# A ViT tower on one core: the second turning of x and a weighing moved on TensorE, the last rows' scores moved on VectorE

## Chip, cores and metric

The kernel runs on one core of one Trainium2 chip. The metric is the time on the device in microseconds, the median of some runs. Times below are microseconds unless ns is written. PE is TensorE (PEld its weight loads), DVE is VectorE, ACT is ScalarE, POOL is GpSimd, SP is the sync engine, which issues most DMAs.

## What is computed

One layer of a vision tower on 32 images of 128 tokens and one class token, 1024 features, in float32:

```
h  = S4D kernels from x, log_dt, A, B               (32, 128, 1024)     "mix"
h  = concat([cls_tok, h], axis=1)                   (32, 129, 1024)
xn = layernorm(h);  q, k, v = xn@Wq.T, xn@Wk.T, xn@Wv.T      32 heads, 8 for k and v, of 32
q, k = rope(q), rope(k);  p = softmax(causal(q k^T / sqrt(32)));  h = h + (p v) @ Wo.T
xn = layernorm(h);  h = h + quant8_per_token(xn) @ quant8_per_channel(w).T + b
```

## The kernel before

Three stages follow each other: the mix (0 to about 165 us), attention (to about 1025 us) and the FFN (to the end). Each engine has its own queue, written out by hand, and the queues meet in semaphores. The order of the work is the order of the code in each engine's `body(t)`.

**Attention** handles one tile (one image, 128 tokens) per `body(t)`; each body has 8 steps `s`. Several tiles are in work at once: in the body of t, the rows of n = t+1 are normalised and turned, q, k and v of t are projected, the scores and the softmax of b = t-1 are made, and its weighing with v belongs to c = t-2 (softmax lags by steps: `group_at(t, s, lag)` gives the group of four heads that is due). The bodies of tiles 4 to 29 run in a hardware loop, the first and last are written out.

- Projection (line 1098): 72 matmuls of 128x128x512 a tile, nine in each step: four at its head (`ahead = 4`), five at its end. float32 is split in two parts (`xT_hi`, `xT_lo`; `w_hi`, `w_lo`) and three products are made.
- `turn_x(n, r)` (line 1130): four transposes of `xn` into one PSUM bank, rounds r = 0 and 1. ACT's `split_x` (1229) casts the bank to `xT_hi`, then DVE's `split_x` (1349) makes `xT_lo` from the bank and `xT_hi` and increments `x_lo`. `x_bank` names the bank: Y_BANK (ps 5) for both rounds, except in the first tiles. `x_steps` gives the steps, 6 and 7.
- `scores` (1141) at steps 1 and 5, each 32 matmuls into four banks. They need q, which is turned (1122) through Y_BANK and copied by ACT (`store_q`, 1215) at steps 0 and 3, and k (1109, 1209).
- On DVE `mask` (1392), `row_maximum` (1401), `inverse` (1408), `part_turned` (1385, the 32x32 transposing of p); on ACT `exponentials` (1223); on POOL `normalise_p` (979). SP writes p in parts to DRAM (`part_p`, 876) and reads it back whole (`whole_p`, 886). `part_turned` of group g waits for the parts of group g-2.
- `weigh(c, half)` (1153) multiplies p with v into C_BANK (ps 4) at steps 3 and 7. ACT's `context` (1248) copies the bank to `ctxo`, SP stores it (844), and POOL's `save_ctx` (984) keeps its last column. At step 7 of POOL, `save_ctx` stands ahead of the normalising of the next step.

In step 7, TensorE issued four projections, `turn_x(n, 1)`, `weigh(c, 1)` and five projections.

**FFN** runs one tile per body too: `project` (1747, 48 matmuls with Wo) of tile t, then `dense_layer` (1839, 16 matmuls) of tile c = t-1 on the int8 values. On DVE a tile's residual and statistics (1884, 1886) come once its projection ends, then `quantise` (1912 to 1925); SP turns the rows with a DMA (1628) before the dense layer. For the first three tiles the projection is made ahead, in the attention stage's last bodies. In between, the last token of all 32 images (it has a 129th key) is handled apart: `end_scores` (1961 to 1969), `end_weights`, `end_context` on DVE.

## Time and profile before

| | |
|---|---|
| runs | 1484.79, 1489.23, 1493.75 us; median 1489.23 |
| profiled execution | 1493.45 us, span of the core 1491.6 us |
| PE busy | 1428.2 us (96%) |
| DVE busy | 1160.9 us (78%) |
| POOL busy | 921.2 us (62%) |
| ACT busy | 734.1 us (49%) |
| DMA | 255.60 MB, mean 171 GB/s |

The profile is of one execution. A chain of work that ended last is followed back from the last instruction; 79% of it lies on PE. Matmuls are pipelined: one starts while the last still runs, so the distance of starts counts, not the duration. A releaser of a wait is inferred from semaphores; "issue" means that none was found.

### The profile page before, as it was taken

To read this page: it belongs to the slowest core of one execution; us is meant where nothing else is said; L and a number is where in the kernel's file an instruction comes from. 1 tells how busy PE (TensorE), PEld (TensorE's weight loads), DVE (VectorE), ACT (ScalarE), POOL (GpSimd) and SP (SyncE) were. 2 spreads that over 40 slices of the span, in tenths; PEclk is the share of its full clock that TensorE was granted. 3 is DMA by queue.
4 is the path that set the end of the run, shared out by engine and by line. 5 is a ranking of instruction groups with operands and counts; after the bars stand their busy time and mean duration, and the time that the engine had idled before them with its cause. 6 is when DMAs were issued, how large, how long until landed. Compare 5 with 4: busy or idle time off the path is not lost.

```text
span 1491.6 us, 34063 instructions
## 1 busy us (share of the span) xinstructions
PE 1428.2 (96%) x10442; PEld 1109.5 (74%) x10442; DVE 1160.9 (78%) x2285; ACT 734.1 (49%) x2673; POOL 921.2 (62%) x958
## 2 busy tenths in 40 slices
PE   5999888999999999999999999889999999999997
PEld 3999866777777777777777777676677777777774
DVE  7888678789999999999999998787765655656555
ACT  6897566576767676676767676562000000000000
POOL 5796156576767767676767767445555556455552
PEclk8999999999999999999999999999999999999998
DMA  9356666677767777777767776867434344343442
GB/s 236 102 142 152 191 142 164 181 191 204 202 200 205 201 210 194 209 194 203 200 196 206 198 206 189 259 207 200 149 113 148 116 130 134 112 145 116 133 113 60
DMA packets 264458, 255.60 MB, mean 171 GB/s; under 512 B 73329, under 2 KB 201586, under 8 KB 264402
## 3 DMA queue, kind: packets, MB, share of 16 engines
q1 hardware_dynamic: 257586, 233.87, 56.4%
q10 hardware_dynamic: 6816, 21.04, 4.7%
q8 instruction: 29, 0.48, 0.1%
q14 instruction: 27, 0.22, 0.1%
HBM read 138.26 MB, written 106.57 MB: 164 GB/s over the span
## 4 chain that ended last, share of the span: by engine, by line
PE 79%; DVE 7%; POOL 6%; DMA 3%; issue 2%; SPq 2%; ACT 1%; ACTq 0%; DVEq 0%; POOLq 0%
PE att_ps L1098 33%; PE ffn_o L1747 22%; PE ffn_y L1839 7%; PE att_ps L1141 4%; PE att_ps L1153 4%; POOL yb L358 3%; PE att_ps L1130 2%; PE att_ps L1122 2%; POOL yb L364 2%; PE mix_ps L447 1%; DMA p_blocks<-pB 1%; SPq L876 1%; PE att_ps L1109 1%; DMA xqT<-xq 1%; DVE m L641 1%
## 5 line engine op out<-in xcount | busy, mean ns | idle before, releaser
L1223 ACT ACTIVATE pr<-sm,ml 128x128 f32<-128x128 f32 x1024 | 399.1, 393 | 164.6 <-DVE ml L1401 163.3
L979 POOL TENSOR_TENSOR pr<-pr,ri 128x512 f32<-128x512 f32 x256 | 266.9, 1043 | 206.9 <-DVE ri L1408 199.8
L1098 PE MATMUL att_ps<-w_lo,xT_hi 128*128 128x512 f32 x776 | 319.9, 412 | 0.0
L1098 PE MATMUL att_ps<-w_hi,xT_hi 128*128 128x512 f32 x776 | 312.5, 403 | 3.9 <-DVE xT_lo L1349 3.1
L1098 PE MATMUL att_ps<-w_hi,xT_lo 128*128 128x512 f32 x776 | 307.6, 396 | 0.0
L1801 ACT CAST cT_hi<-ctx_in 128x512 fp32r<-128x512 f32 x64 | 36.4, 616 | 363.1 <-PE ffn_o L1747 350.8
L1747 PE MATMUL ffn_o<-wo_hi,cT_hi 128*128 128x512 f32 x528 | 211.8, 401 | 2.3 <-DVE wo_lo L1790 1.7
L1392 DVE TENSOR_TENSOR sm<-att_ps,cst 128x512 f32<-128x512 f32 x256 | 170.0, 664 | 51.9 <-PE att_ps L1141 51.9
L1747 PE MATMUL ffn_o<-wo_hi,cT_lo 128*128 128x512 f32 x528 | 205.7, 390 | 0.0
L1747 PE MATMUL ffn_o<-wo_lo,cT_hi 128*128 128x512 f32 x528 | 205.4, 389 | 0.0
L1223 ACT ACTIVATION_READ_ACCUMULATOR pr<-sm,ml 128x1 f32 x1024 | 193.4, 189 | 0.0
L1385 DVE STREAM_TRANSPOSE pB<-pr 128x512 f32<-128x512 f32 x256 | 176.3, 689 | 21.8 <-DMA p_blocks<-pB 19.6
L1401 DVE TENSOR_REDUCE ml<-sm 128x4 f32<-128x512 f32 x256 | 176.1, 688 | 9.1
L1098 PEld LDWEIGHTS att_ps<-w_hi,xT_hi 128*128 128x128 f32 x776 | 146.1, 188 | 41.2 <-issue 2.9
L1098 PEld LDWEIGHTS att_ps<-w_lo,xT_hi 128*128 128x128 f32 x776 | 146.6, 189 | 39.1 <-issue 12.5
L1098 PEld LDWEIGHTS att_ps<-w_hi,xT_lo 128*128 128x128 f32 x776 | 146.7, 189 | 28.6
L1884 DVE TENSOR_TENSOR h<-ffn_o,h_in 128x512 f32<-128x512 f32 x66 | 45.5, 690 | 148.1 <-PE ffn_o L1747 148.1
L1720 POOL TENSOR_TENSOR hb<-h,bias_sb 128x512 f32<-128x512 f32 x66 | 85.5, 1295 | 95.1 <-DVE xq L1925 60.6
L1839 PE MATMUL ffn_y<-wq,xqT 128*128 128x512 bf16 x528 | 124.9, 392 | 10.1 <-DMA xqT<-xq 10.1
L965 POOL TENSOR_SCALAR xn<-hbuf,mv,rstd 128x512 f32<-128x512 f32 x64 | 133.3, 2083 | 0.2
L1747 PEld LDWEIGHTS ffn_o<-wo_hi,cT_hi 128*128 128x128 f32 x528 | 99.2, 188 | 26.3 <-issue 3.6
L447 PE MATMUL mix_ps<-eb,m 128*128 128x128 f32 x1024 | 116.1, 275 | 1.0 <-DVE m L632 0.6
(212 smaller groups left out, 2340.7 us busy)
## 6 DMA issues: line engine op xcount, KB each, us to landing
pT<-p_blocks SPq DMA_DIRECT2D x256, 256.0 KB, 2.9
p_blocks<-pB SPq DMA_DIRECT2D x512, 64.0 KB, 2.0
h_rows<-ho SPq DMA_DIRECT2D x64, 256.0 KB, 3.8
ctx_turned<-ctxo SPq DMA_DIRECT2D x64, 256.0 KB, 3.6
h_in<-h_rows SPq DMA_DIRECT2D x32, 512.0 KB, 3.7
out_dram<-yo SPq DMA_DIRECT2D x32, 512.0 KB, 2.7
ctx_in<-ctx_turned SPq DMA_DIRECT2D x30, 512.0 KB, 3.3
hbuf<-h_rows ACTq DMA_DIRECT2D x29, 512.0 KB, 4.7
```

Source lines behind the costliest of these rows:

```text
L447: mm = nc.tensor.matmul(bank[:, cols], term[:, half, h, slots].rearrange("p j c -> p (j c)"), eb[:, k % 3, half * CH + h, :], start=term i ...
L965: G.tensor_scalar(xn[:, cols], hbuf[:, n[1], cols], mv[:, 0:1], rstd[:], ALU.subtract, ALU.mult).then_inc(xn_ready, 1)
L979: G.tensor_tensor(pr[:, g % 4], pr[:, g % 4], ri[:, g % 2, :].unsqueeze(2).to_broadcast([P, GQ, P]), ALU.mult).then_inc(p_ready, 1)
L1098: mm = nc.tensor.matmul(bank[:], x_part[:, t[1], e, tok:tok + P], w_part[blk][:, e, :], start=(r == 0), stop=(r == EC * 3 - 1))
L1141: mm = nc.tensor.matmul(S_BANK[j][:, q * P:(q + 1) * P], qT[rows, half, q, :], kT[rows, b[1], half, :], start=True, stop=True)
L1223: a = nc.scalar.activation(pr[:, g % 4, q, :], sm[:, g % 2, q, :], ACT.Exp, bias=ml[:, b[1], 0, h:h + 1], accum_out=ml[:, b[1], 1, h:h + 1])
L1385: V.transpose(pB[:, g % 2].rearrange("p k h f -> p h k f"), pr[:, g % 4].rearrange("p h (k f) -> p h k f", k=4)).then_inc(p_turned, 1)
L1392: V.tensor_tensor(sm[:, g % 2], S_BANK[g % 4][:].rearrange("p (q k) -> p q k", q=GQ), cst[:, C_MASK:C_MASK + P].unsqueeze(1).to_broadcast( ...
L1401: V.tensor_reduce(ml[:, b[1], 0, heads_of(g)], sm[:, g % 2], AX.X, ALU.max, negate=True).then_inc(negmax_ready, 1)
L1720: done = nc.gpsimd.tensor_tensor(hb[:, t[1], cols], h1[:, t[1], cols], bias_sb[:, cols], ALU.add)
L1747: mm = nc.tensor.matmul(O_BANK[half][:], c_part[:, t[1], e, :], w_part[:, e, half * BK:(half + 1) * BK], start=(r == 0), stop=(r == PER_HA ...
L1839: mm = nc.tensor.matmul(Y_BANK[half][:], xqT[:, c[1], e, :], wq8[:, e, half * BK:(half + 1) * BK], start=(e == 0), stop=(e == EC - 1))
```

## The change

Five things change in attention. (1) Round 1 of every tile's x goes to C_BANK. (2) From tile 1 on, `turn_x(n, 1)` comes at the end of step 6 instead of the middle of step 7; it now waits for the first context of tile n-3 to be out of the bank. (3) `weigh(c, 1)` goes to the end of step 7, behind its five projections, and waits for both splits of tile n. (4) DVE makes both splits of x at one place, before the mask of step 7; ACT copies the context of half 1 behind the exponentials of step 7. (5) SP stores that half at step 0 of the next body, behind `part_p` and `whole_p`. In the FFN, (6) DVE makes `end_scores` in the body of tile 2, behind `quantise`, instead of at the end of the body of tile 1.

```diff
     def x_bank(n, r):
 
-        return C_BANK if r == 1 and fixed(n) and nth(n) <= 2 else Y_BANK
+        return C_BANK if r == 1 else Y_BANK
...
     def x_steps(n):
 
-        return (3, 4) if at(n, 0) else (6, 7)
+        return (3, 4) if at(n, 0) else (6, 7) if last_rows(n) else (6, None)
...
                 if s == 1 and exists(c, NB):
                     store_ml(c)
-                if s == 7 and exists(c, NB):
+                if s == 0 and exists(shifted(t, -3), NB):
+                    store(shifted(t, -3), 1)
+                if s == 7 and at(t, NB + 1):
                     store(c, 1)
...
         def turn_x(n, r):
             pe.wait_ge(xn_ready, XROUNDS * nth(n) + r + 1)
-            at_least(pe, x_lo, 2 * nth(n) + (r if x_bank(n, r) is Y_BANK else 0))
+            at_least(pe, x_lo, 2 * nth(n))
             at_least(pe, k_stored, number(n))
+            if r == 1 and exists(shifted(n, -3), NB):
+                pe.wait_ge(ctx_ready, 2 * number(shifted(n, -3)) + 1)
...
             at_least(pe, ctx_ready, 2 * u + half)
+            if half == 1 and exists(shifted(b, 3), NB):
+                pe.wait_ge(x_lo, 2 * nth(shifted(b, 3)) + 2)
...
-                if s == 7 and exists(c, NB):
-                    weigh(c, 1)
                 for r in rounds_at(t, s):
                     pe_round(pe, r)
                 if has_rows(t):
                     project(t, min(s * per_step + ahead, count), min((s + 1) * per_step, count))
+                if s == 6 and has_rows(n) and x_steps(n)[1] is None:
+                    turn_x(n, 1)
+                if s == 7 and exists(c, NB):
+                    weigh(c, 1)
...
                 for r in range(XROUNDS):
-                    if s == x_steps(n)[r] and has_rows(n):
+                    if s == (x_steps(n)[r] or 7) and has_rows(n):
                         split_x(n, r)
-                if s == 7 and exists(c, NB):
-                    context(c, 1)
...
                 if exists(d, NB):
                     exponentials(d, g)
+                if s == 7 and exists(c, NB):
+                    context(c, 1)
...
-                if s == x_steps(n)[1] and has_rows(n):
+                if s == (x_steps(n)[1] or 7) and has_rows(n):
                     split_x(n, 0)
+                    if x_steps(n)[1] is None:
+                        split_x(n, 1)
...
             if exists(t, NT):
                 quantise(t)
+            if at(t, 2):
+                end_scores()
             for half in range(2):
                 if exists(c, NT):
                     scale_out(c, half)
                 if last_rows(c):
                     add_last(c, half)
-            if at(t, 1):
-                end_scores()
```

TensorE's queue in the loop, steps 6 and 7 of a body, before (ps 4 is the contexts' bank, ps 5 the other; in brackets the semaphores waited for):

```order
L1098 MATMUL att_ps7<-w_hi2,xT_lo 128x512
L1098 MATMUL att_ps7<-w_hi2,xT_hi 128x512
L1130 MATMUL att_ps5<-cst,xn 128x128 [waits att_k_stored,att_x_lo,att_xn_ready]
L1130 MATMUL att_ps5<-cst,xn 128x128 x3
L1153 MATMUL att_ps4<-pT,v_sb 32x128 [waits ctx_ready,att_v_moved,att_p_whole1]
L1153 MATMUL att_ps4<-pT,v_sb 32x128 x15
L1098 MATMUL att_ps7<-w_lo2,xT_hi 128x512
```

And now (lines are the changed kernel's; seven of the nine projections between are left out):

```order
L1100 MATMUL att_ps7<-w_lo2,xT_hi 128x512
L1100 MATMUL att_ps7<-w_hi2,xT_lo 128x512
L1134 MATMUL att_ps4<-cst,xn 128x128 [waits att_k_stored,ctx_ready,att_x_lo,att_xn_ready]
L1134 MATMUL att_ps4<-cst,xn 128x128 x3
...
L1100 MATMUL att_ps7<-w_lo2,xT_hi 128x512
L1100 MATMUL att_ps7<-w_hi2,xT_lo 128x512
L1159 MATMUL att_ps4<-pT,v_sb 32x128 [waits ctx_ready,att_x_lo,att_v_moved,att_p_whole1]
```

The second turning stands four projections earlier, without need of the first round's split, and the weighing nine projections behind it, with `x_lo` as a new wait.

ScalarE's queue at the same place, before and now (the register rows belong to waits and the loop):

```order
L1223 ACTIVATE pr,ml<-sm,ml 128x128 x4
L1228 REGISTER_ALU
L1229 CAST xT_hi<-att_ps5 128x4x128
L1248 COPY ctxo<-att_ps4 128x512
L1219 REGISTER_ALU
L1223 ACTIVATE pr,ml<-sm,ml 128x128 x4
L816 REGISTER_ALU
L816 COMPARE_AND_BRANCH
L1215 COPY qT<-att_ps5 128x512
L1223 ACTIVATE pr,ml<-sm,ml 128x128 x12
```

```order
L1231 ACTIVATE pr,ml<-sm,ml 128x128 x4
L1236 REGISTER_ALU
L1237 CAST xT_hi<-att_ps4 128x4x128
L1227 REGISTER_ALU
L1231 ACTIVATE pr,ml<-sm,ml 128x128 x4
L1256 COPY ctxo<-att_ps4 128x512
L816 REGISTER_ALU
L816 COMPARE_AND_BRANCH
L1223 COPY qT<-att_ps5 128x512
L1231 ACTIVATE pr,ml<-sm,ml 128x128 x12
```

The copy of the context, which stood ahead of step 7's four exponentials, stands behind them, right before the copy of q (`qT`).

VectorE's queue in the FFN, bodies of tiles 1 and 2, before and now:

```order
L1925 TENSOR_SCALAR xq<-xr 128x1024
L1935 SCALAR_TENSOR_TENSOR ya<-ffn_y,xs,w_scale 128x512 x2
L1961 TENSOR_TENSOR prod<-ffn_c,k_end 32x512 x2
L1965 TENSOR_REDUCE s_end<-prod 32x32
L1967 SCALAR_TENSOR_TENSOR nm_end<-s_end,ml_end 32x32
L1968 TENSOR_TENSOR w_end<-nm_end,ml_end 32x32
L1969 TENSOR_TENSOR w_end<-nm_end,s_end 32x32
L1884 TENSOR_TENSOR h<-ffn_o,h_in 128x512
L1886 BN_STATS ffn_st<-h 128x6
```

```order
L1945 SCALAR_TENSOR_TENSOR ya<-ffn_y,xs,w_scale 128x512 x2
L1894 TENSOR_TENSOR h<-ffn_o,h_in 128x512
...
L1935 TENSOR_SCALAR xq<-xr 128x1024
L1971 TENSOR_TENSOR prod<-ffn_c,k_end 32x512 x2
L1975 TENSOR_REDUCE s_end<-prod 32x32
L1977 SCALAR_TENSOR_TENSOR nm_end<-s_end,ml_end 32x32
L1978 TENSOR_TENSOR w_end<-nm_end,ml_end 32x32
L1979 TENSOR_TENSOR w_end<-nm_end,s_end 32x32
L1945 SCALAR_TENSOR_TENSOR ya<-ffn_y,xs,w_scale 128x512 x2
L1983 TENSOR_TENSOR e_end<-e_end,ml_end 32x32
```

The five instructions of the last rows' scores (`prod` to `w_end`) stood between the scaling of tile 0 and the residual of tile 2; now they stand behind tile 2's quantising (`xq`).

## Rows read from the trace of the kernel before

**Rows 1.** The page, busy time of the matmuls over the whole span
```profile
PE 1428.2 (96%) x10442; PEld 1109.5 (74%) x10442; DVE 1160.9 (78%) x2285; ACT 734.1 (49%) x2673; POOL 921.2 (62%) x958
```

**Rows 2.** Waits of 320 to 900 us: total, times, longest
```profile
DVE sm L1392 <- PE att_ps L1141: 38.6, 48, 0.9
...
PEld att_ps L1130 <- issue: 13.8, 24, 1.2
```

**Rows 3.** Timeline of PE, one tile: start, duration (us), instruction
```profile
581.93 1.17 PE L1141 MATMUL att_ps<-kT,qT 32*128 32x128 f32 x32
...
597.67 0.60 PE L1130 MATMUL att_ps<-cst,xn 128*128 128x128 f32 x4
...
598.34 0.39 PE L1098 MATMUL att_ps<-w_hi,xT_lo 128*128 128x512 f32 x1
...
599.96 0.40 PE L1098 MATMUL att_ps<-w_hi,xT_hi 128*128 128x512 f32 x1
600.52 0.63 PE L1130 MATMUL att_ps<-cst,xn 128*128 128x128 f32 x4 [0.16 <-issue]
...
606.00 1.17 PE L1141 MATMUL att_ps<-kT,qT 32*128 32x128 f32 x32
```

**Rows 4.** Timeline of DVE, the same tile
```profile
599.76 0.65 DVE L1349 TENSOR_TENSOR xT_lo<-att_ps,xT_hi 128x512 fp32r<-128x512 f32 x1
...
601.80 0.69 DVE L1349 TENSOR_TENSOR xT_lo<-att_ps,xT_hi 128x512 fp32r<-128x512 f32 x1
...
607.34 0.69 DVE L1392 TENSOR_TENSOR sm<-att_ps,cst 128x512 f32<-128x512 f32 x1 [0.92 <-PE att_ps L1141]
```

**Rows 5.** Timeline of ACT, the same tile
```profile
598.79 0.40 ACT L1223 ACTIVATE pr<-sm,ml 128x128 f32<-128x128 f32 x1
...
600.25 0.19 ACT L1223 ACTIVATION_READ_ACCUMULATOR pr<-sm,ml 128x1 f32 x1
...
602.22 0.59 ACT L1248 COPY ctxo<-att_ps 128x512 f32<-128x512 f32 x1 [0.46 <-PE att_ps L1153]
...
605.03 0.59 ACT L1215 COPY qT<-att_ps 128x512 f32<-128x512 f32 x1 [0.67 <-PE att_ps L1122]
```

**Rows 6.** Timeline of POOL, the same tile
```profile
602.98 0.19 POOL L984 COPY c_end<-ctxo 128x4 f32 x1 [1.38 <-ACT ctxo L1248]
603.13 1.04 POOL L979 TENSOR_TENSOR pr<-pr,ri 128x512 f32<-128x512 f32 x1
```

**Rows 7.** Chain that ended last, first tiles: start, us, what
```profile
282.35 2.27 issue
...
309.88 1.19 issue
```

**Rows 8.** Busy time by stretches: length, PE, PEld, DVE, ACT, POOL, granted clock, DMA
```profile
283.00:290.00 7.00, 5.38 (x48) 4.17 (x49) 6.30 (x13) 3.41 (x14) 3.51 (x4) 0.76 0.51 135
...
1049.00:1057.00 8.00, 7.28 (x25) 3.23 (x26) 7.02 (x13) 0.00 (x0) 2.33 (x3) 0.58 0.36 135
```

**Rows 9.** Timeline of PE, dense layers of FFN tiles 2 and 3
```profile
1049.72 6.56 PE L1839 MATMUL ffn_y<-wq,xqT 128*128 128x512 bf16 x16 [2.83 <-DMA xqT<-xq]
...
1067.93 3.63 PE L1839 MATMUL ffn_y<-wq,xqT 128*128 128x512 bf16 x16
```

**Rows 10.** Timeline of DVE, start and end of the last rows' scores
```profile
1031.97 1.27 DVE L1961 TENSOR_TENSOR prod<-ffn_c,k_end 32x512 f32<-32x512 f32 x2
...
1034.94 0.67 DVE L1884 TENSOR_TENSOR h<-ffn_o,h_in 128x512 f32<-128x512 f32 x1
```

**Rows 11.** Timeline of SP, turned rows of FFN tiles 2 and 3 issued
```profile
1043.14 1.67 SPq L1628 DMA_TRANSPOSE xqT<-xq  x1
...
1058.66 1.24 SPq L1628 DMA_TRANSPOSE xqT<-xq  x1
```

**Rows 12.** Landing of the turned rows (line 1628), 1010 to 1120 us
```profile
DMA to landing us min/median/max: 4.1/5.0/6.7
```

**Rows 13.** Landing of the parts of p (line 876), 320 to 900 us
```profile
DMA to landing us min/median/max: 1.7/2.1/2.9
```

## The prediction

> **What bounds the kernel now.** I read the page first: the matmuls are busy 96% of the span [rows 1], so the time is the length of TensorE's own queue plus the holes in it. Then the waits of 320 to 900 us, the regular part of the attention stage (24 tiles): there TensorE has one hole of size per tile, before a turning of x (line 1130), 13.8 us in 24 times as its weight loads show it, and VectorE waits twice per tile for the scores, 0.8 us a time [rows 2]. So TensorE leads, and VectorE follows with little slack.
>
> The timeline of one tile shows the hole. The reader is to see where the even step breaks: seven projection matmuls lie between 598.34 and 599.96, so one takes 0.231 us. The next instruction should begin at 600.19, and the second turning begins at 600.52 [rows 3]. It writes the bank that VectorE reads in its first split of x, from 599.76 to 600.41 [rows 4], and starts 0.11 us behind it. The hole is 0.33 us, and "issue" in the brackets hides that it is a semaphore of VectorE. From scores to scores, 581.93 to 606.00, a tile takes 24.07 us [rows 3].
>
> The first tiles are worse: the same place costs 2.27 us and two tiles later 1.19 us in the chain [rows 7] (the tile before the former lost 2.03 alike, the one behind the latter 0.81). After the long one the granted clock of the next 7 us averages 0.76, that is a time at 1.2 instead of 2.4 GHz [rows 8]; after the one of 1.19 the turning ran at its full speed.
>
> **The change in a steady tile, step by step.** (1) The second turning goes to the contexts' bank, so it no longer waits for the first split. The 0.33 us are gone on TensorE. It also moves four matmuls ahead, to 600.19 - 4 x 0.231 = 599.27. Its other waits are met: the bank's earlier content is copied out and xn normalised microseconds before.
>
> (2) The weighing now comes nine matmuls later. A turning between two projections costs 598.34 - 597.67 - 0.231 = 0.44 us [rows 3], so it wants to start at 599.27 + 0.44 + 9 x 0.231 + 0.08 = 601.87. It waits for VectorE's second split. ScalarE casts that half behind its exponentials, 0.09 us after 600.25, for 0.59 us [rows 5], so until 600.93; the split then ends at 600.95 + 0.69 = 601.64 (0.69 from [rows 4]). That is 0.2 us early, so I cost it at nothing; it is the thinnest cover here.
>
> (3) VectorE does both splits in a row and idles for the cast from 600.41 to 600.95. From the first split's start to the second's there were 2.04 us in the trace [rows 4]: the split (0.6), a mask and a row maximum (1.4). Both now come behind the second split, whose successor starts 0.6 us after it, at 601.56: the row maximum ends at 602.96, where VectorE was free again at 601.80 + 0.61 = 602.41 with the split done. So the rest of its queue shifts by some 0.45 us on its own account: it had finished a transposing of p (0.68 us) at 607.34 - 0.92 = 606.42 [rows 4] and now would at 606.87.
>
> (4) ScalarE's four exponentials of step 7 start at 603.0. A group takes 600.25 + 0.09 - 598.79 = 1.55 us [rows 5]; then the context is copied (one copy follows another after 0.48 us), and the copy of q starts at 605.03. Today it starts at 605.03 too, waiting for TensorE [rows 5]. So q is stored at 605.6, and the scores can start at 605.66, where TensorE's own path alone gives 606.00 - 0.33 = 605.67 or a little less. Two chains end together; the gain is 0.34 us at most, if nothing adds.
>
> (5) POOL still saves a column of the context in step 7, and behind it in its queue stands the normalising of p. Today the column is saved at 602.98, 0.17 us behind the copy's end, and p normalised from 603.13, for 1.04 us [rows 5, 6]; now the copy ends at 605.12, the column follows at 605.29, and p is normalised from 605.44 to 606.48. VectorE's transposing of that p starts at 606.52 instead of 606.19, and its mask comes 0.63 us later, at 607.15, where the earlier scores would allow 607.34 - 0.34 = 607.00 [rows 4]. That 0.15 us is taken from the 0.8 us of slack that VectorE has before the next scores [rows 2], and costs nothing.
>
> (6) On SP the store of the context's second half goes behind the parts and the whole of the next step of p. Part 5 of p is issued about 0.9 us later relative to the scores; parts land in 2.1 us, 2.9 at most [rows 13], and VectorE needs it 3 us after its issue has ended. Nothing.
>
> The new waits on registers (ctx_ready at the turning, x_lo at the weighing) have no row; the nearest is the weights' idle time of a turning without a hole, under 0.1 us. Between 0 and 0.2 us per tile, I take 0.04. So **0.30 us a tile**, 25 tiles: 7.5 us. Bounds: 0.41 us (TensorE alone, if q comes earlier) and 0.10.
>
> (7) The first four tiles that the new bank reaches. In the second, the old turning stood from 282.35 to 284.62. The weighing would stand 0.44 + 5 x 0.231 = 1.6 us behind the old place, at 283.95, and its split ends 0.6 us behind the old release, at 285.2. So 1.2 us of waiting remain of 2.27, and the clock should stay up, as it did after 1.19 us. The low clock cost 7 x (1 - 0.76) = 1.7 us [rows 8], so 2.8 us come back, less what step (4) takes: 2.5 here, and 2.5 in the tile before. In the next two the weighing finds its split done and the stalls of 1.19 and 0.81 go: 1.9 us. Together **6.9 us** (bounds 4 and 7.5; the lower one if the clock still falls).
>
> (8) The last attention tile runs into a stretch where VectorE is bound by the landing of p's parts; there part 5 is late by what steps (3) and (5) add. **Minus 0.4 us.**
>
> **The scores of the last rows.** Their five instructions hold VectorE from 1031.97 to 1034.94 [rows 10], ahead of the residual, statistics and quantising of the third tile, and its dense layer waits for exactly that: TensorE idles 2.83 us until 1049.72 [rows 9]. Moved behind, they take 2.97 us off this way. SP issued the turned rows at 1043.14 [rows 11]; its queue has a few small loads first, so 1040.6. The dense layer starts at 1047.1, 2.6 us earlier. Its 16 matmuls took 6.56 us at a mean clock of 0.58 where the next tile's took 3.63 [rows 8, 9]; with an idle time under 1 us they should run at full speed: 2.9 us more, 5.5 in all. But it isn't all kept. VectorE's sum of work up to the fourth tile's quantising is unchanged, so its turned rows still leave at 1058.66 [rows 11] and land 4.1 to 6.7 us later, 5.0 in the middle [rows 12]: at 1063.7. TensorE now arrives at 1067.93 - 5.5 = 1062.4. It waits 1.3 us; **4.3 us** stay. Bounds: 5.5 (landing in 4.1), and nothing, if they land in 6.7 at 1065.4 and the dense layer falls to the low clock again (2.5 less 2.9).
>
> Here a rule speaks against the change. The trace shows that the clock fell after idle times of 2.27 and 2.83 us and not after 1.19 [rows 7 to 9], and my sum keeps it up in both places. The Trainium skill, page "TensorE: Matmul & The Clock Gate", Part 1, has the gate follow how busy the array has recently been, not one idle time; by that, several short holes in a row could bring it down as one long one does.
>
> **The sum.** 7.5 + 6.9 - 0.4 + 4.3 = 18.3 us. The profiled execution took 1493.45 us, so 1475.1 for its like; the median of the runs is 1489.23, so **1471 us**.
>
> **Rivals.** (A) ScalarE's chain sets the tile. If steps (3) and (4) take 0.3 us more than counted (a wait's latency on each of four hand-overs), the scores start where they do today and the steady gain is nil; the copy of q was waiting for TensorE until now, which speaks against it, the exact tie for it. 4.0 + 3.0 = 7 us: 1482. 15%.
> (B) The clock rule above: the holes of 1.2 and 1.3 us still bring it down. 4.0 of 6.9 and 1.4 of 4.3 stay: 7.5 + 4.0 - 0.4 + 1.4 = 12.5 us: 1477. 10%.
> (C) Slower: part 5 of p. In the regular stretch parts land in 2.1 us, but in the first tiles VectorE did wait for them. If the later issue makes it wait, each tile loses what exceeds 0.9 + 0.8 us of slack; at a landing of 4.8 us that is 1.0 us a tile, 25 us, against 18 gained: 1496. It decides from a landing of about 4 us; the longest in 24 tiles was 2.9. 4%.
> (D) The hole is not the split but the sequencer working through waits ("issue"). Then the change gives only the scores' 4.3 us and adds two waits at 0.1 us to 30 tiles: 1488. Against it: the first turning has the same three waits and no hole. 3%.
>
> **Chances.** Forecast 68%, A 15, B 10, C 4, D 3. A measurement of this kernel tells 0.5%, 7.4 us, from no change (the limit is 1481.8). Faster: forecast, B and half of A, 0.86. Same: the other half of A and D, 0.10. Slower: C, 0.04. The range runs from all upper bounds, 0.41 x 25 + 7.5 + 5.5 = 23 us and some spread of the runs, 1463, to A's far end, 1484.
>
> **What would show it.** No idle time before the second turning; the weighing 0 to 0.2 us behind its place; the copy of q at the same distance from its scores as TensorE's arrival; a tile of 23.77 us instead of 24.07; 0.3 us waits of VectorE for POOL's p; the clock at 1.00 in the second tile and in the dense layer of the third; the dense layer near 1047 minus what the attention stage saved. A tile of 24.0 or more, with TensorE waiting for the copy of q, would make A right; a wait of VectorE for parts of p in most tiles, C.

## The result, and the profile after

| | before | changed |
|---|---|---|
| median of 8 runs each | 1489.22 us | 1477.13 us |
| lowest and highest | 1484.79, 1493.75 | 1475.51, 1481.45 |
| profiled execution (span) | 1493.45 (1491.6) | 1476.76 (1475.0) |
| PE busy | 1428.2 us | 1418.8 us |

The ratio is 0.9921, 95% interval 0.9905 to 0.9938: the change saves 12 us, 9 to 14 by the interval. The same kernel on another chip, beside the last two experiments, gave 0.9917 (0.9894 to 0.9940). The forecast was 1471 us with a range of 1463 to 1484: faster was right, the range holds it, and the gain is a third smaller than the forecast's 18.3.

TensorE's matmuls cover 96% of the span as before [rows 1]:

```profile
PE 1418.8 (96%) x10442; PEld 1109.0 (75%) x10442; DVE 1162.4 (79%) x2285; ACT 725.4 (49%) x2673; POOL 920.2 (62%) x958
```

**The steady tiles.** The waits of 320 to 900 us, by engine and line: us in total, times, the longest. They answer to [rows 2].

```profile
POOL c_end L986 <- ACT ctxo L1256: 83.1, 24, 3.7
...
DVE sm L1400 <- PE att_ps L1145: 11.5, 25, 0.7
...
PEld att_ps L1145 <- ACT qT L1223: 8.9, 24, 0.5
DVE pB L1393 <- POOL pr L981: 7.8, 24, 0.4
DVE xT_lo L1357 <- ACT xT_hi L1237: 7.3, 17, 0.5
DVE pB L1393 <- DMA p_blocks<-pB: 3.9, 14, 0.4
```

The wait of the turning's weights ("issue", 13.8 us in 24 times) is gone, and VectorE waits for the scores 11.5 us instead of 38.6: it has lost two thirds of its slack. In its place stand two small waits that the forecast had named: VectorE's for POOL's p (7.8 us in 24 times, 0.33 a time) and its wait for the cast of x's second half (7.3 us in 17 times).

One tile of TensorE, as in [rows 3]; a line is a group's start, its duration and the instruction:

```profile
583.98 1.17 PE L1145 MATMUL att_ps<-kT,qT 32*128 32x128 f32 x32
...
590.03 0.60 PE L1134 MATMUL att_ps<-cst,xn 128*128 128x128 f32 x4
...
592.65 1.08 PE L1159 MATMUL att_ps<-pT,v_sb 128*32 128x128 f32 x32
...
594.69 0.60 PE L1124 MATMUL att_ps<-cst,rsq 128*128 128x128 f32 x4
...
596.38 1.17 PE L1145 MATMUL att_ps<-kT,qT 32*128 32x128 f32 x32
```

No idle time stands behind any of them: TensorE's queue of the tile has no hole left. The second turning at 590.03 used to wait for a split; the weighing at 592.65 finds its split done, though only just (the splits, two of them, end at 590.87 + 1.48 = 592.35 in the row below). ScalarE, POOL and VectorE beside it, each with its own idle time in brackets [rows 4 to 6]:

```profile
593.71 0.40 ACT L1231 ACTIVATE pr<-sm,ml 128x128 f32<-128x128 f32 x1 [2.08 <-DVE ml L1409]
...
595.26 0.56 ACT L1256 COPY ctxo<-att_ps 128x512 f32<-128x512 f32 x1
595.73 0.58 ACT L1223 COPY qT<-att_ps 128x512 f32<-128x512 f32 x1
```

```profile
595.99 0.19 POOL L986 COPY c_end<-ctxo 128x4 f32 x1 [3.28 <-ACT ctxo L1256]
596.14 2.04 POOL L981 TENSOR_TENSOR pr<-pr,ri 128x512 f32<-128x512 f32 x2
```

```profile
590.87 1.48 DVE L1357 TENSOR_TENSOR xT_lo<-att_ps,xT_hi 128x512 fp32r<-128x512 f32 x2
...
597.22 0.71 DVE L1393 STREAM_TRANSPOSE pB<-pr 128x512 f32<-128x512 f32 x1 [0.22 <-POOL pr L981]
```

The copy of q starts at 595.73, ends at 596.31, and its scores start at 596.38, the tie of step (4). Before, ScalarE stood idle ahead of that copy and waited for TensorE (0.67 us in [rows 5]); that wait is gone from the list. The matmuls don't wait there. Their weight loads wait for ScalarE, 8.9 us in 24 times in the waits above, but in the kernel before it was 8.7 in 24 times, so that wait says nothing of the tie; the experiment context_first below does. POOL sits idle for 3.28 us until the context is copied, and VectorE's transposing waits 0.22 us for the p behind it, as step (5) has it.

A tile's length is best taken over many. The group of 32 scores is issued 64 times; from the 13th to the 59th lie 23 tiles:

| | 13th scores | 59th scores | us a tile |
|---|---|---|---|
| before | 365.33 | 918.81 | 24.06 |
| changed | 359.38 | 904.53 | 23.70 |

The gain is 0.36 us a tile, 8.3 us over these 23. Of it 0.33 us is the hole. Another 0.03 is the second turning itself: its four transposes take 0.60 us now (590.03 above) and took 0.63 behind the hole [rows 3]. In the two further traces with the old attention it came back as 24.05, in the five further ones with the changed attention as 23.70 each time.

**The first tiles.** TensorE's largest hole there is now this, and the clock behind it is the second row (columns as in [rows 8]):

```profile
282.51 1.08 PE L1159 MATMUL att_ps<-pT,v_sb 128*32 128x128 f32 x32 [2.14 <-DVE xT_lo L1357]
```

```profile
282.00:290.00 8.00, 7.49 (x82) 5.93 (x83) 6.45 (x14) 4.25 (x18) 4.56 (x6) 0.79 0.76 223
```

It is the hole that the forecast wanted to shrink to 1.2 us, and the clock fell as in the kernel before. VectorE is late for it by waits of its own, in the 10 us ahead:

```profile
273.39 0.71 DVE L1393 STREAM_TRANSPOSE pB<-pr 128x512 f32<-128x512 f32 x1 [1.85 <-POOL pr L981]
...
277.24 0.71 DVE L1393 STREAM_TRANSPOSE pB<-pr 128x512 f32<-128x512 f32 x1 [1.75 <-DMA p_blocks<-pB]
...
281.12 1.25 DVE L1357 TENSOR_TENSOR xT_lo<-att_ps,xT_hi 128x512 fp32r<-128x512 f32 x2
```

**The last rows' scores.** TensorE's dense layers of FFN tiles 2 and 3, then VectorE's quantising and scores, then SP's queue and the landing of the turned rows of tile 2. They answer to [rows 9 to 12].

```profile
1035.38 5.02 PE L1849 MATMUL ffn_y<-wq,xqT 128*128 128x512 bf16 x16 [4.91 <-DMA xqT<-xq]
...
1052.05 3.63 PE L1849 MATMUL ffn_y<-wq,xqT 128*128 128x512 bf16 x16
```

```profile
1023.58 0.69 DVE L1935 TENSOR_SCALAR xq<-xr 128x1024 bf16<-128x1024 f32 x1
1024.18 1.27 DVE L1971 TENSOR_TENSOR prod<-ffn_c,k_end 32x512 f32<-32x512 f32 x2
...
1034.58 0.69 DVE L1894 TENSOR_TENSOR h<-ffn_o,h_in 128x512 f32<-128x512 f32 x1
```

```profile
1019.47 3.34 SPq L1673 DMA_DIRECT2D ctx_last_rows<-cls_value  x4
1022.91 1.48 SPq L1599 DMA_DIRECT2D ctx_in<-ctx_turned  x1
1024.50 0.87 SPq L1604 DMA_DIRECT2D h_in<-h_rows  x1
1025.43 3.72 SPq L1638 DMA_TRANSPOSE xqT<-xq  x1
```

```profile
DMA to landing us min/median/max: 9.9/9.9/9.9
```

The scores (1024.18) did leave the way of the quantising (1023.58). But the turned rows, which landed 6.5 us after their issue in the kernel before, now need 9.9, and TensorE idles 4.91 us instead of 2.83. The dense layer took 5.02 us instead of 6.56. Set against the last weighing, at 1024.85 before and 1010.25 now, tile 2's dense layer starts after 24.87 us before and 25.13 now, so no sooner, and tile 3's after 43.08 and 41.80. The stretch is 1.3 us shorter, and what made it so is that tile 2's matmuls ran 1.5 us faster, not that they began earlier.

### The profile page after: what moved, and what is told of

Its sections match the earlier page's. It is cut to its first block, busy times and chain, and to the rows that moved or that the text cites. A ratio compares the mean times of both kernels' runs of the same rounds, so it can differ in the third digit from the quotient of the medians.

```text
span 1475.0 us, 34108 instructions
## 1 busy us (share of the span) xinstructions
PE 1418.8 (96%) x10442; PEld 1109.0 (75%) x10442; DVE 1162.4 (79%) x2285; ACT 725.4 (49%) x2673; POOL 920.2 (62%) x958
## 4 chain that ended last, share of the span: by engine, by line
PE 72%; DVE 8%; POOL 6%; DMA 4%; SPq 4%; issue 3%; ACT 2%; ACTq 0%; DVEq 0%; POOLq 0%
PE att_ps L1100 30%; PE ffn_o L1757 21%; PE ffn_y L1849 7%; PE att_ps L1145 4%; PE att_ps L1159 3%; POOL yb L358 3%; SPq L876 3%; DMA p_blocks<-pB 2%; PE att_ps L1124 2%; POOL yb L364 2%; PE att_ps L1134 2%; PE mix_ps L447 1%; DMA xqT<-xq 1%; DVE sm L1400 1%; DVE pB L1393 1%
## 5 line engine op out<-in xcount | busy, mean ns | idle before, releaser
L1100 PE MATMUL att_ps<-w_hi,xT_hi 128*128 128x512 f32 x776 | 318.9, 411 | 2.6 <-DVE xT_lo L1357 2.0
L1100 PE MATMUL att_ps<-w_lo,xT_hi 128*128 128x512 f32 x776 | 316.5, 408 | 0.0
L1894 DVE TENSOR_TENSOR h<-ffn_o,h_in 128x512 f32<-128x512 f32 x66 | 45.5, 690 | 147.8 <-PE ffn_o L1757 147.7
L1757 PEld LDWEIGHTS ffn_o<-wo_hi,cT_hi 128*128 128x128 f32 x528 | 99.2, 188 | 25.3 <-ACT wo_hi L1795 1.8
```

Of the source, the lines that this page charges most:

```text
L1100: mm = nc.tensor.matmul(bank[:], x_part[:, t[1], e, tok:tok + P], w_part[blk][:, e, :], start=(r == 0), stop=(r == EC * 3 - 1))
L1757: mm = nc.tensor.matmul(O_BANK[half][:], c_part[:, t[1], e, :], w_part[:, e, half * BK:(half + 1) * BK], start=(r == 0), stop=(r == PER_HA ...
```

## The experiments

Eleven kernels ran in three groups, each group beside runs of the kernel before on its chip (their medians: 1491.1, 1491.4 and 1490.4 us). Besides the ratio I read two lengths from each trace, which scatter less than the time: the steady tile, and the way from the start of the last weighing to tile 3's dense layer, called the FFN way below.

| kernel | median, us | ratio (95%) | steady tile | FFN way |
|---|---|---|---|---|
| before, profiled with the result | 1489.22 | 1 | 24.06 | 43.08 |
| changed, profiled with the result | 1477.13 | 0.9921 (0.9905 to 0.9938) | 23.70 | 41.80 |
| changed_again | 1478.05 | 0.9917 (0.9894 to 0.9940) | 23.70 | 42.67 |
| scores_back | 1479.21 | 0.9928 (0.9908 to 0.9948) | 23.70 | 43.65 |
| scores_only | 1492.64 | 1.0004 (0.9986 to 1.0021) | 24.05 | 40.97 |
| copies_later | 1475.57 | 0.9901 (0.9880 to 0.9923) | 23.70 | 37.41 |
| copies_later_again | 1474.97 | 0.9901 (0.9879 to 0.9923) | 23.70 | 37.68 |
| before_copies_later | 1486.78 | 0.9976 (0.9962 to 0.9989) | 24.05 | 37.42 |
| copies_scores_back | 1476.15 | 0.9897 (0.9872 to 0.9921) | 23.70 | 38.36 |
| turning_later | 1493.18 | 1.0011 (0.9996 to 1.0025) | 24.24 | 42.14 |
| context_first | 1480.90 | 0.9919 (0.9897 to 0.9941) | 23.77 | 43.80 |
| save_later | 1479.45 | 0.9924 (0.9899 to 0.9948) | 23.70 | 42.32 |
| two_products_out | 1469.58 | 0.9844 (0.9820 to 0.9868) | 23.32 | 42.04 |

In the traces of the last four kernels of the table the record of a dense layer's first matmul is missing, so that their FFN way is read one matmul, 0.23 us, too long.

My theory after the result: the attention part of the change works by taking every hole out of TensorE's queue; the scores' move works too, but its gain is lost to the landing of the turned rows, which is set by four copies of small pieces queued ahead of them on SP (line 1673). The rivals are the forecast's own figure (4.3 us for the scores) and, for the attention, that VectorE or ScalarE sets the tile.

### The two parts, each by itself

scores_back takes one part out of the changed kernel, scores_only puts it alone into the kernel before:

```
-            if at(t, 2):
-                end_scores()
             for half in range(2):
...
+            if at(t, 1):
+                end_scores()
```

> The changed kernel with the last rows' scores back behind the second tile's scaled product; the change to the attention stays. The forecast's theory (the scores' move is worth 4.3 us, since xqT of tile 2 lands as much earlier as it is issued earlier) gives 1477.1 + 4.3 = 1481.4 us. My theory now: the landing is bound by what is queued ahead of it, the four copies of cls_value into ctx_last_rows and then ctx_in and h_in (xqT landed 9.9 us after its issue in the changed kernel, 6.5 us before), so that an issue 2 to 3 us later lands at the same moment, the dense layer of tile 2 still starts about 1035.4 us and the time is 1477 to 1479 us. In the trace: landing of that xqT near 7 us instead of 9.9.

> The kernel before with the scores' move alone. The forecast's theory: 1489.2 - 4.3 = 1484.9 us. My theory now (landing bound by the small copies ahead of it): 1487.5 to 1489.2 us, and xqT of tile 2, issued about 1040.5 us instead of 1043.1, lands about 9 us later, at the moment at which it landed before.

The part back, the ratio is 0.9928 against 0.9921; alone, it is 1.0004. By both, the scores are worth nothing that the times can tell, and 4.3 us of 1489 is a ratio of 0.9971, outside scores_only's interval. The turned rows of tile 2 landed 8.2 us after their issue in scores_back, 8.7 in scores_only. I had expected 7 and 9: the issue that comes later does land faster, but not by as much. The FFN ways say the same: 43.65 to 41.80 and 42.67 in the changed kernel (1.4 us), 43.08 to 40.97 in the kernel before (2.1 us), where 4.3 was forecast. These sizes are rough. Three kernels below have the FFN of the changed kernel too, context_first, save_later and two_products_out, and their ways are 43.6, 42.1 and 41.8 (less the 0.23 us named under the table), so that one trace scatters by as much as what is to be measured. Tile 2's dense layer starts 25.60 us after the last weighing in scores_back and 25.0 to 26.0 in the five traces with the attention changed and the scores moved: the move doesn't bring it forward. All this also shows that nearly the whole measured gain is the attention's.

### The copies ahead of the turned rows

```
-            if at(t, 2):
+            if at(t, 3):
                 sp.wait_ge(v0_out, 16)
                 for q in range(GQ):
                     sp.dma_start(tail_dram[NB:P].rearrange("t (g q d) -> t g q d", g=HKV, q=GQ)[:, :, q, :],
```

> The changed kernel with the four copies of cls_value into ctx_last_rows issued one tile later, behind the turning of tile 2's xq. My theory: ctx_in, h_in and xqT are no longer queued behind them, xqT of tile 2 is issued about 1 us earlier (1024.4) and lands in 4 to 5 us as the others do, before tile 2's projection ends (1030.5), so the dense layer starts with no hole (4.9 us in the changed kernel), at full clock (3.6 us instead of 5.0). That is up to 4.9 + 1.4 = 6.3 us; some of it can be lost to the wait of the tile after: 1471 to 1474 us. Rival: the landing is long because of ctx_in and h_in themselves (1 MB ahead of it) and the copies cost nothing: 1477 us, landing still 8 us or more.

> The kernel before with only the four copies of cls_value issued one tile later. My theory: xqT of tile 2, issued at 1043.1 us as before, lands after 4.4 us instead of 6.5, the hole ahead of the dense layer shrinks from 2.8 to 0.7 us and its clock stays full (3.6 us instead of 6.6): 2.1 + 2.9 = 5 us, 1484 to 1486 us. Rival (the copies cost nothing): 1489 us.

The four copies are of 96 KB each, in pieces of 32 floats (128 bytes). The same stretch of SP and TensorE with them behind:

```profile
1020.29 0.37 SPq L1599 DMA_DIRECT2D ctx_in<-ctx_turned  x1
1025.06 0.33 SPq L1604 DMA_DIRECT2D h_in<-h_rows  x1
1025.43 1.25 SPq L1638 DMA_TRANSPOSE xqT<-xq  x1
...
1032.28 3.43 SPq L1673 DMA_DIRECT2D ctx_last_rows<-cls_value  x4
```

```profile
DMA to landing us min/median/max: 4.4/4.4/4.4
```

```profile
1031.05 3.63 PE L1849 MATMUL ffn_y<-wq,xqT 128*128 128x512 bf16 x16
...
1048.42 3.62 PE L1849 MATMUL ffn_y<-wq,xqT 128*128 128x512 bf16 x16 [1.15 <-DMA xqT<-xq]
```

The turned rows leave at the same moment, 1025.43, and land after 4.4 us instead of 9.9; tile 2's dense layer starts with no hole and takes 3.63 us. Why, the bandwidth shows. Here are 40 slices of 1022 to 1031 us, busy tenths of the 16 engines and GB/s, first of the changed kernel, then of copies_later:

```profile
DMA  3033323332333233223220110211222268989899
GB/s 51 13 58 50 50 48 58 61 51 48 59 61 51 48 59 60 49 48 52 43 31 15 32 25 15 36 18 23 45 45 42 39 142 261 370 327 464 346 473 401
```

```profile
DMA  7998897110000000015689896889899200200000
GB/s 200 273 382 328 328 473 310 55 55 18 0 0 0 0 0 0 0 55 127 182 309 492 273 382 218 270 231 214 162 272 298 47 0 0 73 0 0 0 0 0
```

With the copies in the queue it moves about 50 GB/s for 4.5 us, then less until 1029; the 512 KB each of ctx_in and h_in, and the turned rows behind them, wait until it is nearly over (the last copy lands at 1030.6) and then go at 260 to 470. The Trainium skill, page "DMA: Bandwidth & Descriptors", section "Queues, rings and completion order", says that each DMA engine takes the descriptors of one ring in their order; the trace agrees, since three transfers issued from 1022.9 to 1025.4 hardly move before the copies are through.

In the changed kernel this is worth 4.4 to 5.3 us of the FFN way (41.80 and 42.67 to 37.41), in the kernel before 5.7 us. In time it is 3 us: 1478.05 and 1474.97 on one chip, and 0.9901 twice against 0.9921 and 0.9917. The intervals of these overlap; that of before_copies_later against its kernel does not reach 1. The rival was that the 1 MB of loads ahead makes the landing long. The loads are still issued ahead of the turned rows, and the 512 KB of h_in only 0.37 us ahead, without harm; the 512 KB of ctx_in have landed by then, since SP gets to them sooner without the copies. So the copies are the cause, directly and by holding the loads back. How the 5 us divide between the two isn't shown.

I had expected 1471 to 1474 us for copies_later, and 1475.57 came. The next hole takes a part back, as said there: 1.15 us before tile 3's dense layer. For before_copies_later I had expected 1484 to 1486 us against 1489. 1486.78 came, against 1491.1 on that chip: 4.3 us less by the medians and 3.6 by the ratio, where 5 was expected. Its turned rows landed after 4.2 us instead of 6.5, and the dense layer took 3.63, as expected.

### Both together: what the scores' move is worth without the copies

The edits of scores_back and of copies_later in one kernel, beside the changed kernel and copies_later once more.

> The changed kernel with the four copies of cls_value one tile later and the last rows' scores back where they were. My theory: with the copies out of the way the place of the scores is worth nothing or up to 1 us, since then VectorE's and the tensor engine's own work sets the tile: tile 3's dense layer starts 37.4 to 38.4 us after the last weighing (37.4 with the copies moved alone, with either place of the scores), 1473 to 1477 us. Rival (the forecast's): the scores ahead of tile 2's quantising cost 2.6 us wherever the copies are: 40 us after the last weighing, 4.3 us more than with the copies moved alone.

> The changed kernel once more, beside the two that follow, so that they are compared on one chip. 1477 to 1480 us (0.990 to 0.994 of before); steady tile 23.70 us; xqT of tile 2 lands 9 to 10 us after its issue, and tile 3's dense layer starts 41.5 to 42.5 us after the last weighing.

> The changed kernel with the four copies one tile later, once more, beside the changed kernel: 3 to 4.5 us under it (41.8 - 37.4 = 4.4 us between the last weighing and tile 3's dense layer), 1473 to 1476 us.

The FFN way is 38.36 us, against 37.41 and 37.68: 0.7 to 1.0 us for the place of the scores, and the ratios (0.9897, 0.9901) are the same. Tile 2's dense layer has a hole of 1.95 us ahead of it, tile 3's then none. So the forecast's 4.3 us fail here too: VectorE had room for most of the 3 us of scores. The times of the other two are those expected, 3.1 us apart. The FFN way of the changed kernel again, 42.67, lies 0.2 above the stretch I had given. The turned rows landed after 10.0 us there, as in the first trace.

### The bank without the earlier place

turning_later keeps the new bank, the split of both halves in one go and the weighing at the end of step 7, but puts the turning itself back:

```
                 for r in range(XROUNDS):
-                    if s == x_steps(n)[r] and has_rows(n):
+                    if s == (x_steps(n)[r] or 7) and has_rows(n):
                         turn_x(n, r)
...
-                if s == 6 and has_rows(n) and x_steps(n)[1] is None:
-                    turn_x(n, 1)
```

> The changed kernel with x's second turning back in step 7, behind four products of the projection as in the kernel before; the bank stays the contexts', the split stays one group of two, and the weighing stays at the end of step 7. It tells the bank from the place. The turning comes four products later (some 0.95 us), about 591.0 instead of 590.0 in the tile read; ScalarE's cast then ends about 592.3 instead of 591.6, VectorE's second split about 593.0 instead of 592.3, and the weighing, which the tensor engine reaches at 592.65, waits 0.3 to 0.8 us for it; the mask behind the split is as late. My theory: the tile takes 24.0 to 24.4 us instead of 23.70 (the kernel before: 24.06), in all 8 to 17 us over the changed kernel: 1485 to 1494 us. Rival: the bank alone brings the gain, the place is indifferent: 1477 us.

```profile
DVE xT_lo L1355 <- ACT xT_hi L1235: 20.5, 24, 1.1
...
PE att_ps L1159 <- DVE xT_lo L1355: 7.9, 24, 0.3
```

24.24 us a tile, more than the kernel before (24.06). The new wait of the weighing for the second split stands in it 24 times with 0.33 us, just where the old hole of 0.33 was, and VectorE waits 20.5 us for the cast instead of 7.3. So the attention change without the earlier place is a loss of 0.18 us a tile against the kernel before; what pays is that the turning comes four products earlier, into a bank that lets it. (The kernel before with the new bank and nothing else did not run, nor did the weighing's place or the order of the splits by itself.) The 0.54 us over the changed kernel stand in two places, read from the starts of the matmuls in 23 tiles. From the last product to the weighing it is 0.72 us instead of 0.33. From the last product to the scores behind q's copy it is 0.45 instead of 0.33. The time, 1493.18 us, lies in the expected 1485 to 1494.

### Relief off TensorE, and less work on it

context_first puts ScalarE's copy of the context ahead of step 7's exponentials; save_later puts POOL's column of it behind the next normalising of p:

```
+                if s == 7 and exists(c, NB):
+                    context(c, 1)
                 for r in rounds_at(t, s):
...
                     exponentials(d, g)
-                if s == 7 and exists(c, NB):
-                    context(c, 1)
```

```
                     normalise_p(d, g)
+                if s == 0 and exists(shifted(t, -3), NB):
+                    save_ctx(shifted(t, -3), 1)
...
-                if s == 7 and exists(c, NB) and not at(c, NB - 1):
-                    save_ctx(c, 1)
```

> The changed kernel with ScalarE's context copy of the second half back ahead of step 7's exponentials. The weighing ends (593.73) just when those exponentials can start (593.71), so the copy pushes them 0.5 us back and comes 1.5 us earlier itself; the copy of q after both starts where it did. My theory: nothing changes in the steady tile (23.70 us, 0 to 0.1 more) and the time stays at 1477 to 1479 us; the order on ScalarE was indifferent, though GpSimd gets the context 1.5 us earlier and VectorE's wait of 0.22 us for pr goes. Rival: exponentials later by 0.5 us make the chain to the next scores later by as much: 24.2 us a tile, 1489 us.

> The changed kernel with GpSimd's save of the second half's last context column behind the first normalising of the next tile, so that pr no longer waits behind ctxo (3.28 us idle on GpSimd, 0.22 us on VectorE in each tile). My theory: the tensor engine has no hole left in the steady tile, so relief of VectorE and GpSimd is worth nothing there: 23.70 us a tile, 1476 to 1478 us. Rival: VectorE still sets the tile (its wait of 0.22 us is on the path): 23.48 us a tile, 24 x 0.22 = 5 us less, 1472 us.

The waits of save_later, where POOL no longer stands behind the context:

```profile
POOL c_end L986 <- ACT ctxo L1256: 26.8, 24, 1.1
DVE sm L1400 <- PE att_ps L1145: 17.6, 24, 0.8
...
DVE pB L1393 <- DMA p_blocks<-pB: 2.4, 3, 1.0
```

POOL's idle time for the context falls from 83.1 to 26.8 us, VectorE's for p (7.8 us) is gone, its wait for the scores grows from 11.5 to 17.6, and the tile stays at 23.70. The 0.22 us were slack turned into slack. (The median, 1479.45, lies above the expected 1476 to 1478; the ratio, 0.9924, is the changed kernel's.) context_first has 23.77: 0.07 more, within what I had written, so the order on ScalarE that the change brings is all but indifferent. The 0.07 stand in one place, the scores behind q's copy, which start 0.39 us after the last product instead of 0.33. There ScalarE has no slack left: the tie of step (4) is real. (Its median, 1480.9, lies above the 1479 I had given; its first scores came at 215.32 us, the latest but one of all the traces of this study, and its ratio is the changed kernel's.)

two_products_out removes work from TensorE alone, two products of the projection in each tile:

```
+                if not last_rows(t) and blk == 2 and r in (5, 8):
+                    continue
                 x_part, w_part = PARTS[part]
```

> The changed kernel with two of the 72 products of each tile's projection left out (in the third block: one of w_lo with xT_hi and one of w_hi with xT_lo are missing from q's second half), to see whether the tensor engine's queue sets the steady tile now. Each product takes 0.23 us in the queue. My theory: it does, so the tile takes 23.70 - 0.46 = 23.24 us, and over 32 tiles the time falls by 13 to 15 us, to 1462 to 1464 us; a part of it can be lost to the next engine, since VectorE's chain is only some 0.1 to 0.4 us behind. Rival: another engine (VectorE, or ScalarE's copy of q in front of the scores) sets it: 23.6 to 23.7 us a tile, 1475 to 1477 us.

```profile
L1147 PE MATMUL att_ps<-kT,qT 32*128 32x128 f32 x1600 | 58.7, 283 | 1.0
L1161 PE MATMUL att_ps<-pT,v_sb 128*32 128x128 f32 x1568 | 53.0, 275 | 1.3 <-DVE xT_lo L1359 0.9
```

23.32 us a tile: 0.38 of the 0.46 us come through, and the rest is idle time in the last column, 1.0 us before the scores and 1.3 before the weighing (0.7 of the latter in one of the first tiles). By the starts, the scores behind q's copy come 0.41 us after the last product instead of 0.33, and the weighing 0.37 instead of 0.33. So TensorE sets the tile, the rival is out, and the reserve behind it is thin: ScalarE's copy of q and VectorE's split show as soon as 0.4 us is taken. In time it is 8 us (of the medians) to 11 us (of the ratios) under the changed kernel, less than the 13 to 15 I had given, which took all 32 tiles at 0.46; 0.38 for the 24 steady ones alone gives 9.

## Why the forecast was right, and where not

**Steady tile, steps (1) to (6): right, by its own mechanism.** 0.36 us instead of 0.30, inside the bounds of 0.10 and 0.41. The hole is gone, the weighing finds its split done, ScalarE's copy of q and TensorE arrive together, and VectorE waits for POOL's p at no cost, as save_later shows. The 0.04 us I had set aside for the new waits weren't needed, and 0.03 came from the turning itself, which I had not counted. 23 tiles give 8.3 us.

**First four tiles, step (7), 6.9 us: mis-sized, about 3.9.** Here are the six tiles from the first scores to the 13th, each from scores to scores, in three traces with the old attention (before, scores_only, before_copies_later) and in six with the changed one (changed, changed_again, scores_back and the three with the copies later or both). The forecast's four tiles are numbers 2 to 5.

| tile | 1 | 2 | 3 | 4 | 5 | 6 | sum |
|---|---|---|---|---|---|---|---|
| old | 22.6, 24.1, 25.5 | 28.3, 25.0, 24.1 | 27.6, 27.9, 28.3 | 25.1, 25.0, 26.1 | 24.8, 24.2, 24.1 | 24.0, 24.1, 24.1 | 152.3, 150.2, 152.1 |
| changed | 22.3 to 23.9 | 23.8 to 24.3 | 25.3 to 27.5 | 23.9 to 25.3 | 23.7 to 25.6 | 23.7 | 144.5 to 147.7 |
| gain of the means | 1.1 | 1.8 | 1.7 | 0.4 | 0.0 | 0.4 | 5.4 |
| forecast | 0.3 | 2.5 | 2.5 | 1.9 for both | | 0.3 | 7.5 |

Two sentences failed. The larger miss is "In the next two the weighing finds its split done and the stalls of 1.19 and 0.81 go: 1.9 us." In five of the six changed traces the weighing of tile 4 waits 1.0 to 1.4 us for its split; the trace of the result, where it doesn't, is the exception. In those five VectorE had stood 1.8 to 2.1 us for the landing of p's parts some 5 us earlier, as here in copies_later:

```profile
303.70 0.71 DVE L1393 STREAM_TRANSPOSE pB<-pr 128x512 f32<-128x512 f32 x1 [2.10 <-DMA p_blocks<-pB]
```

```profile
308.97 1.08 PE L1159 MATMUL att_ps<-pT,v_sb 128*32 128x128 f32 x32 [1.38 <-DVE xT_lo L1357]
```

That the wait for the parts causes the hole is read from the order of the rows; no run took it away. The other sentence is "So 1.2 us of waiting remain of 2.27, and the clock should stay up", with 2.5 us for each of two tiles. In tile 3 the hole is 1.35 to 2.14 us, and the clock stayed at 1.00 in four of the six traces but fell in two, the trace of the result among them. And tile 2's 2.5 us were read off one execution: it took 28.3 us there, but 25.0 and 24.1 in the other two traces of the old attention. (A reading to be corrected too: the hole of 1.19 us is one tile behind that of 2.27, not two.)

**Last attention tile, step (8), minus 0.4 us: open.** From the 59th scores to the last weighing the three old traces take 106.0, 109.7 and 106.0 us, the six changed ones 104.1 to 107.6. The scatter hides it.

**The last rows' scores, 4.3 us: the step that failed.** The sentence is "its queue has a few small loads first, so 1040.6. The dense layer starts at 1047.1": it carried the landing of 6.5 us over to an earlier issue. The 6.5 was already at the far end of 4.1, 5.0 and 6.7 [rows 12], and the reason, four copies issued from 1034.97 to 1038.40 ahead of it in SP's queue, stood a few rows above in the same timeline. What the runs showed: issued 3.1 us earlier against the last weighing, the turned rows landed after 9.9 us instead of 6.5 and so no earlier. Measured on the FFN way: some 1.4 us in the changed kernel and 2.1 in the old one, at most 1.0 without the copies. The second half of the term, "with an idle time under 1 us they should run at full speed", never came to be tested by the change, since the hole grew to 4.91 us; with the copies moved it holds (3.63 us behind holes of 0 to 1.95). The lower bound, nothing, was right to be in the range; the mechanism behind it was not the one I gave.

**From the sum to the median.** The forecast took its sum off the profiled execution (1493.45) and shifted the rest to the median, so 1475.1 for an execution like the profiled one, and 1476.76 came. The two profiled executions differ by 16.7 us: 6.1 in the first six tiles, 8.3 in the next 23, 0.3 up to the last weighing, 1.3 in the FFN way and 0.7 behind it, while the first scores come at 213.0 and 213.2 us. The median fell by less, 12.1 us, since the profiled execution of the kernel before lay 4.2 us above its median and the changed one at its own; which stretch held these 4.2 us isn't known. What the parts give in the mean of the traces, 5.4 + 8.3 + 1.4 = 15.1 us, is 3 us more than the medians and 1 to 6 more by the interval; I can't say which part gives them back. That the total fell inside the range does not confirm the terms: the first tiles and the scores were too large, the last tile is open, and the steady tile alone came out as worked out.

**The rivals.** (A), 1482, ScalarE's chain: out, since the steady gain is there. (B), 1477, has the right number for the wrong reason: it let holes of 1.2 and 1.3 us bring the clock down. In the first tiles, behind the first scores, the clock stayed at 1.00 after every hole of 0.7 to 1.74 us in all the traces, and after 1.95 us in the FFN of copies_scores_back. It did fall in both places of the trace of the result, but behind holes of 2.14 and 4.91 us. (C): in the steady tiles VectorE's wait for parts of p is 3.9 us in 14 times, 0.4 at most, so the later store costs nothing there; in the first tiles the same wait, 1.8 to 2.1 us a time, stands ahead of the holes that stayed. (D) is out with the steady tile. (Its sum was off as well: two waits of 0.1 us in 30 tiles are 6 us, so 1491, not 1488.)

## What to carry to other kernels

Before a step is moved so that a transfer leaves earlier, look at what stands ahead of that transfer in its queue: four copies of small pieces held 1 MB of loads and the turned rows for 5 us, and moving them by one tile brought more than moving 3 us of VectorE's work. When an instruction is moved into another buffer, ask whether it also comes earlier; the change without the earlier place made each tile 0.18 us longer. And a sum made from one execution should take from it only what recurs tile by tile: its holes at the start are partly its own, as tile 2 with 28.3, 25.0 and 24.1 us shows.

## What the chip did that I had not expected

The clock doesn't follow the length of a hole alone. In the attention's first tiles, counted from behind the first scores, the mean granted clock of 8 us behind a hole was 0.79 to 0.81, part of it at 1.2 instead of 2.4 GHz, after holes of 1.94, 2.03, 2.05, 2.14, 2.27, 2.41, 2.46 and 2.85 us, and 1.00 after 1.94, 2.20 and 2.49 us and after every hole shorter than 1.94. The length 1.94 is in both lists: at the same place, at 282 us, the clock fell in copies_scores_back (first row) and not in changed_again (second). The third row, of before_copies_later, follows the hole of 2.20 us:

```profile
282.00:290.00 8.00, 7.97 (x84) 6.32 (x85) 6.44 (x13) 4.25 (x18) 4.05 (x6) 0.79 0.84 231
```

```profile
282.00:290.00 8.00, 7.85 (x90) 6.24 (x91) 7.69 (x15) 5.24 (x24) 4.14 (x6) 1.00 0.78 231
```

```profile
309.00:317.00 8.00, 7.52 (x90) 5.99 (x91) 6.94 (x14) 4.86 (x19) 4.88 (x6) 1.00 0.83 240
```

In the FFN the same dense layer took 6.56 us behind a hole of 2.83, 6.44 behind 4.45, 5.31 behind 3.51 and 5.02 behind 4.91 and 4.82, where 3.63 is its length at full clock: the longer hole was not the dearer one. The Trainium skill, page "TensorE: Matmul & The Clock Gate", Part 1, lets the gate go by how busy the array has been lately; these rows agree in so far as the length of one hole doesn't decide, and no run here shows more of it.

A transfer's landing time is no property of the transfer alone. The turning of tile 2's rows took 4.2 to 5.7 us with the copies out of its way, and 6.5 to 10.0 behind them. Mostly it took longer the sooner it was issued after them, but not by that alone: issued 6.0 us behind the last copy's issue it took 6.5 us in the kernel before and 8.2 in scores_back.
